# Two tiles alone over all columns, pair operands laid out by sample, and one engine for the pair products' banks

## Chip, cores, metric

The kernel runs on one core of a Trainium2 chip. The metric is the device time of one execution in microseconds. Before the change the median of 3 runs is 491.37 us (489.37 to 493.07). TensorE multiplies, VectorE and ScalarE work elementwise, GpSimd issues the gathers, and SyncE's queue issues the other transfers.

## The reference, cut to what matters

```python
field_idx = jnp.arange(26)
sparse_embed = emb_tables[field_idx[None, :], x_sparse]   # [1024, 26, 64]
z = sparse_embed.reshape(1024, 26 * 64)
gram = jnp.einsum('bik,bjk->bij', sparse_embed, sparse_embed)
inner = gram[:, iu, ju]                                   # 325 pairs i < j
dnn_in = jnp.concatenate([x_dense, z, inner], axis=-1)    # [1024, 13 + 1664 + 325 = 2002]
h = jax.nn.relu(dnn_in @ w1 + b1)                         # w1 [2002, 2002]
out = jax.nn.sigmoid(h @ w2 + b2)                         # w2 [2002, 1]
```

All inputs are fp32. Each sample gathers 26 rows of 64 numbers. The pairwise dot products of those rows, the rows themselves and 13 dense features are the input of a layer of 2002 x 2002 and then of one output.

## The kernel before

**Tiling.** The 1024 samples are eight tiles of 128. The 2002 columns of w1 are two halves of 1002 columns (502 + 500, with two columns shared). The contraction of 2002 rows and the bias is 16 pieces of 128: k = 0 to 12 are z (two fields each), k = 13 to 15 are the *tail* (325 pairs, 13 dense features, a one for the bias). To keep fp32 accuracy each operand is split into a high and a low part of type f32r, and TensorE does three products: x_hi x w_hi, x_hi x w_lo, x_lo x w_hi (lines 361, 362, 345).

**Steps and turns.** A *step* is two tiles and one half: its four accumulators fill four PSUM banks, acc0 to acc3. There are 8 steps. A *turn* is what TensorE does with one piece of weights. Most turns are twelve matmuls (two tiles, two chunks of columns, three products). Step 0 is different: its first 11 pieces are used for tile 0 alone and then loaded again for tile 1 alone (22 turns of six matmuls), since tile 1 is gathered later. That gives 139 turns (TURN, line 63).

**Weights.** SyncE loads a piece into one of four slots of w_raw (line 225), ScalarE rounds it to w_hi (line 396), VectorE subtracts for w_lo (line 474); both have six slots. ScalarE and VectorE do this four turns ahead of its use (LEAD).

**What a tile goes through besides.** Five kinds of parts, written as letters in the code:
- T: GpSimd gathers one field of 128 samples in one indirect transfer (line 267); TensorE transposes them two fields at a time into a side bank (line 297), ScalarE writes x_hi from it (line 401), VectorE x_lo (line 481). In four batches a tile.
- O: operands for the pair products. ScalarE writes the high half of the partitions of pair_u and pair_v (lines 412, 413), VectorE the low half (lines 495, 497).
- G: pair products. One matmul takes four samples at once, 4 samples x 32 fields as weights and 4 x 26 as moving operand (line 312). Four matmuls fill a side bank, eight banks make a tile. The banks are evicted, only the diagonal blocks, by ScalarE (even banks, line 425) and VectorE (odd banks, line 509), four copies each.
- R: VectorE transposes the products in blocks of 32 x 32 and adds the two halves into the tail with 25 short additions (lines 520, 524).
- X: TensorE transposes the tail, ScalarE and VectorE split it.

There are four side banks, used in turn; a part that writes one waits until the fourth use before it has been read.

**Order.** Nothing is scheduled at run time. The table PLAN gives every part a place: the whole number is the turn after whose multiply TensorE does it, a fraction under .5 is early, others late. On ScalarE and VectorE the early parts of turn u come before the splits that `ahead(u)` lists for that turn, the late ones behind them. Every engine runs its queue strictly in order. WARM places short matmuls that produce nothing.

## Time and profile before

| | |
|---|---|
| median of 3 runs | 491.37 us (489.37 to 493.07) |
| profiled execution | 491.99 us, span 490.2 us |
| mean granted clock of TensorE | 0.965 |
| TensorE busy | 464.1 us, 95% |
| VectorE busy | 324.7 us, 66% |
| ScalarE busy | 251.0 us, 51% |
| GpSimd busy | 243.3 us, 50% |
| loaded from HBM | 77.87 MB |

How to read it: the span is the time from the first to the last instruction of the profiled execution. Busy is the time in which an engine executes; TensorE's matmuls overlap, so the distance of their starts says more than their duration. A row names the line of the kernel, the engine, the operation and the tiles it writes and reads. PEclk is the clock granted to TensorE, 1.00 is 2.4 GHz and 0.50 is 1.2 GHz.

### The profile page before, as it was taken

To read this page: it belongs to the slowest core of one execution; us is meant where nothing else is said; L and a number is where in the kernel's file an instruction comes from. 1 tells how busy PE (TensorE), PEld (TensorE's weight loads), DVE (VectorE), ACT (ScalarE), POOL (GpSimd) and SP (SyncE) were. 2 spreads that over 40 slices of the span, in tenths; PEclk is the share of its full clock that TensorE was granted. 3 is DMA by queue.
4 is the path that set the end of the run, shared out by engine and by line. 5 is a ranking of instruction groups with operands and counts; after the bars stand their busy time and mean duration, and the time that the engine had idled before them with its cause. 6 is when DMAs were issued, how large, how long until landed. Compare 5 with 4: busy or idle time off the path is not lost.

```text
span 490.2 us, 6190 instructions
## 1 busy us (share of the span) xinstructions
PE 464.1 (95%) x2113; PEld 396.6 (81%) x2113; DVE 324.7 (66%) x724; ACT 251.0 (51%) x438; POOL 243.3 (50%) x215
## 2 busy tenths in 40 slices
PE   8669888999999999999999999999999999999996
PEld 8557876978888888888878888889788878888884
DVE  3457698678575975787577677876876694446422
ACT  2457558448352854385537553764386443433311
POOL 5777787778788888778788878200000000000000
PEclk9889699689989999998999999999999999999999
DMA  6968657655756775487546855562546347556400
GB/s 158 269 188 242 148 136 217 163 109 130 189 129 170 207 190 129 122 208 203 130 114 173 234 140 149 158 218 84 161 149 180 93 156 246 167 164 212 150 3 0
DMA packets 28751, 78.29 MB, mean 160 GB/s; under 512 B 7696, under 2 KB 7704, under 8 KB 28720
## 3 DMA queue, kind: packets, MB, share of 16 engines
q1 hardware_dynamic: 22064, 71.07, 46.2%
q0 software_dynamic: 6656, 6.83, 11.5%
q8 instruction: 17, 0.28, 0.2%
q14 instruction: 14, 0.11, 0.1%
HBM read 77.87 MB, written 0.00 MB: 159 GB/s over the span
## 4 chain that ended last, share of the span: by engine, by line
PE 71%; POOL 16%; issue 6%; DVE 5%; DMA 1%; ACT 0%; ACTq 0%
PE acc L361 20%; PE acc L362 20%; PE acc L345 20%; POOL z L267 16%; PE side L312 9%; PE side L297 2%; DVE tail L524 1%; DVE square L520 1%; DVE gram L509 1%; DMA z<-in_L_rec_emb_tables_dram,idx 1%; DMA idx<-in_r_x_sparse_dram 1%; DVE weighed L552 1%; PE side L322 1%; ACT L449 0%; DVE w_lo L474 0%
## 5 line engine op out<-in xcount | busy, mean ns | idle before, releaser
L267 POOL DMA_INDIRECT z<-in_L_rec_emb_tables_dram,idx x208 | 242.4, 1165 | 66.5 <-issue 63.1
L361 PE MATMUL acc<-w_hi,x_hi 128*128 128x502 f32 (+3 forms) x512 | 208.0, 406 | 1.4 <-ACT x_hi L401 1.3
L362 PE MATMUL acc<-w_lo,x_hi 128*128 128x502 f32 (+3 forms) x512 | 203.0, 396 | 0.0
L474 DVE TENSOR_TENSOR w_lo<-w_raw,w_hi 128x1002 fp32r<-128x1002 f32 (+1 forms) x139 | 164.1, 1201 | 45.1 <-ACT w_hi L396 44.0
L396 ACT CAST w_hi<-w_raw 128x1002 fp32r<-128x1002 f32 (+1 forms) x139 | 140.3, 1031 | 52.2 <-PE acc L345 47.1
L345 PE MATMUL acc<-w_hi,x_lo 128*128 128x502 f32 (+3 forms) x512 | 145.6, 395 | 0.0
L361 PEld LDWEIGHTS acc<-w_hi,x_hi 128*128 128x128 f32 (+1 forms) x512 | 99.1, 194 | 21.1 <-issue 1.9
L345 PEld LDWEIGHTS acc<-w_hi,x_lo 128*128 128x128 f32 (+1 forms) x512 | 98.7, 193 | 20.4
L362 PEld LDWEIGHTS acc<-w_lo,x_hi 128*128 128x128 f32 (+1 forms) x512 | 98.8, 193 | 18.3
L312 PEld LDWEIGHTS side<-pair_v,pair_u 128*128 128x128 f32 x256 | 67.5, 346 | 2.4 <-issue 1.5
L509 DVE COPY gram<-side 32x104 f32<-32x104 f32 x128 | 33.5, 262 | 52.9 <-PE side L312 51.6
L312 PE MATMUL side<-pair_v,pair_u 128*128 128x104 f32 x256 | 66.6, 438 | 1.1 <-DVE pair_v L497 1.1
L425 ACT COPY gram<-side 32x104 f32<-32x104 f32 x128 | 30.6, 239 | 71.3 <-PE side L312 70.2
L401 ACT CAST x_hi<-side 128x512 fp32r<-128x512 f32 (+2 forms) x32 | 16.2, 507 | 74.4 <-PE side L297 74.3
L481 DVE TENSOR_TENSOR x_lo<-side,x_hi 128x512 fp32r<-128x512 f32 (+2 forms) x32 | 18.8, 590 | 37.6 <-ACT x_hi L401 37.4
L412 ACT ACTIVATE pair_v<-x_hi 64x512 fp32r<-64x512 f32 (+2 forms) x64 | 35.1, 549 | 0.4
L413 ACT CAST pair_u<-x_hi 64x512 fp32r<-64x512 f32 (+2 forms) x64 | 33.5, 524 | 0.0
L552 DVE SCALAR_TENSOR_TENSOR weighed<-acc,w2b 128x502 f32<-128x502 f32 (+1 forms) x32 | 20.7, 677 | 16.7 <-PE acc L345 16.6
L297 PE MATMUL side<-ident,z 128*128 128x128 f32 x104 | 17.5, 287 | 12.5 <-DMA z<-in_L_rec_emb_tables_dram,idx 12.5
L495 DVE CAST pair_u<-x_lo 64x512 fp32r<-64x512 f32 (+2 forms) x64 | 27.9, 437 | 1.4
L297 PEld LDWEIGHTS side<-ident,z 128*128 128x128 f32 x104 | 13.4, 147 | 17.8 <-DMA z<-in_L_rec_emb_tables_dram,idx 14.8
L497 DVE CAST pair_v<-x_hi 64x512 fp32r<-64x512 f32 (+2 forms) x64 | 26.7, 417 | 0.0
(33 smaller groups left out, 111.0 us busy)
## 6 DMA issues: line engine op xcount, KB each, us to landing
w_raw<-in_L_rec_w_dram SPq DMA_DIRECT2D x131, 501.0 KB, 4.3
z<-in_L_rec_emb_tables_dram,idx POOLq DMA_INDIRECT x208, 4.0
w_raw<-in_L_rec_w_dram SPq DMA_DIRECT2D x8, 270.1 KB
w2b<-in_L_rec_w_dram SPq DMA_DIRECT2D x1, 501.0 KB, 7.0
w2b<-in_L_rec_w_dram SPq DMA_DIRECT2D x1, 500.0 KB, 8.9
w_raw<-in_L_rec_w_dram SPq DMA_DIRECT2D x8, 50.9 KB
w_raw<-in_L_rec_b_dram SPq DMA_DIRECT2D x8, 3.9 KB
idx<-in_r_x_sparse_dram SPq DMA_DIRECT2D x1, 104.0 KB, 2.7
```

The costliest lines, as they stand in the source:

```text
L267: pool.indirect_dma_start(out=z[:, t % 2, K * f:K * (f + 1)], out_offset=None, in_=emb_rows, in_offset=bass.IndirectOffsetOnAxis(ap=idx[:, ...
L297: last = nc.tensor.transpose(bank(("T", t, q))[:, P * j:P * (j + 1)], z[:, t % 2, P * (first + j):P * (first + j + 1)], ident[:])
L312: last = nc.tensor.matmul(bank(("G", t, q))[0:SIDES * QUAD, wide * g:wide * (g + 1)], pair_u[:, :, :, b].rearrange("p s f -> p (s f)"), pa ...
L345: last = nc.tensor.matmul(o, x_lo[0:rows, t % XS, k, :], wh, start=False, stop=k == KT - 1)
L361: nc.tensor.matmul(o, hi, wh, start=k == 0, stop=False)
L362: nc.tensor.matmul(o, hi, wl, start=False, stop=False)
L396: nc.scalar.copy(w_hi[0:rows, slot, :], w_raw[0:rows, m % RAW, :]).then_inc(w_hi_done, 1)
L412: nc.scalar.mul(pair_v[0:K, f, :], high, 0.5)
L413: last = nc.scalar.copy(pair_u[0:K, :, f, :].rearrange("p s f b -> p f s b"), high.rearrange("p f (s b) -> p f s b", s=SIDES))
L425: last = nc.scalar.copy(gram[rows, at, :], of.rearrange("p (m j) -> p m j", m=GB)[:, :, FIELDS * s:FIELDS * (s + 1)])
L474: nc.vector.tensor_tensor(w_lo[0:rows, slot, :], w_raw[0:rows, m % RAW, :], w_hi[0:rows, slot, :], ALU.subtract).then_inc(w_lo_done, 1)
L509: last = nc.vector.tensor_copy(gram[rows, at, :], of.rearrange("p (m j) -> p m j", m=GB)[:, :, FIELDS * s:FIELDS * (s + 1)])
```

## The change

Three things are changed.

1. **Steps.** Tiles 0 and 1 are each a step of their own over both halves: one tile, four chunks of columns, again four accumulators and twelve matmuls a turn. A piece of weights is then 2002 columns wide and is loaded and split in one go. The other six tiles go in pairs and by halves as before. There are 128 turns: 32 wide and 96 as before. w_raw has six half slots in place of four, so it holds three wide pieces or six narrow ones, like w_hi and w_lo. Wide pieces are split two turns ahead of their use, narrow ones four. Tile 0 is transposed in eight batches (1, 1, 2, 2, 2, 2, 2, 1 pieces), the others in batches of 4, 4, 4 and 1. The WARM matmuls are gone; 36 matmuls in place of 48 stand before the first turn.
2. **Pair operands.** pair_u and pair_v are laid out by sample: for each of 32 groups of four samples, 128 numbers in a row (4 samples x 32 places, of which 26 are fields and six are zero). A pair product reads both operands packed and writes 128 columns instead of 104. The copies that write the operands (O) read x_hi and x_lo with a stride and write four fields next to each other.
3. **Eviction.** ScalarE evicts all eight banks of a tile. VectorE evicts none.

The table PLAN is written anew. The diff, cut to its core:

```diff
-    BATCHES = [(0, 3), (3, 4), (7, 4), (11, FP - 11)]
+    SOLO = 2
+    STEPS = [([t], list(range(HALVES))) for t in range(SOLO)]
+    STEPS += [([g + b for b in range(GROUP)], [h]) for g in range(SOLO, TILES, GROUP) for h in range(HALVES)]
+    PARTED = [(0, 4), (4, 4), (8, 4), (12, FP - 12)]
+    BATCHES = [PARTED] * TILES
+    BATCHES[0] = [(0, 1), (1, 1), (2, 2), (4, 2), (6, 2), (8, 2), (10, 2), (12, FP - 12)]
...
-    RAW = 4
+    RAW = 6
     SPL = 6
-    ALONE = 11
-    WARM_UP = 48
-    LEAD = 4
+    WARM_UP = 36
...
-    STEPS = HALVES * TILES // GROUP
-    TURN = [(0, k, [t]) for t in range(GROUP) for k in range(ALONE)]
-    TURN += [(0, k, list(range(GROUP))) for k in range(ALONE, KT)]
-    for n in range(1, STEPS):
-        TURN += [(n, k, [n // HALVES * GROUP + b for b in range(GROUP)]) for k in range(KT)]
+    TURN = [(n, k) for n in range(len(STEPS)) for k in range(KT)]
     TURNS = len(TURN)
+    WIDE = [len(STEPS[n][1]) for n, _ in TURN]
+    START = [sum(WIDE[:m]) for m in range(TURNS + 1)]
+    def before(m, ring):
+        last = START[m + 1] - 1 - ring
+        return max([u for u in range(m) if START[u] <= last], default=-1)
...
-        ([-1, 2, 6, 10], [0.5, 3.5, 7.5, 10.1],
-         [10.6, 10.6, 10.6, 10.6, 10.6, 10.6, 10.6, 10.6], [12.5], [13.5]),
-        ([10.8, 13, 16, 19], [11.6, 14.5, 18.5, 21.1],
-         [21.5, 21.5, 21.5, 21.5, 21.6, 21.6, 21.6, 21.6], [22.8], [23.7]),
-        ([22.8, 22.9, 24.9, 26.9], [24.3, 26, 27, 29],
-         [30.1, 30.1, 31.1, 31.1, 32.1, 32.1, 32.1, 32.1], [33.1], [35.5]),
...
+        ([-1, 0, 1, 2, 4, 6, 8, 9], [4.5, 7, 10, 10.5],
+         [10.6, 10.6, 10.6, 10.6, 10.6, 10.6, 11, 11], [11.5], [12.1]),
+        ([13, 15, 18, 19], [15.5, 17.5, 20, 21],
+         [22, 22, 22.5, 22.5, 23, 23, 23.5, 23.5], [24.5], [26]),
+        ([26, 28, 29, 30], [28.5, 30.5, 32, 33],
+         [34, 34, 34.5, 34.5, 35, 35, 35.5, 35.5], [36.5], [38]),
...
-    WARM = [(2.1, 5), (6.1, 5), (10.2, 9), (12.2, 1), (13.1, 5), (17.1, 4), (20.1, 6), (21.1, 5),
-            (23.2, 8)]
...
-        pair_u = sb("pair_u", [P, SIDES, QUAD, APART], f32r)
-        pair_v = sb("pair_v", [P, FIELDS, P], f32r)
+        pair_u = sb("pair_u", [P, APART, SIDES, QUAD], f32r)
+        pair_v = sb("pair_v", [P, APART, SIDES, QUAD], f32r)
...
-        w_raw = sb("w_raw", [P, RAW, HW], fp32)
-        w_hi = sb("w_hi", [P, SPL, HW], f32r)
-        w_lo = sb("w_lo", [P, SPL, HW], f32r)
+        w_raw = sb("w_raw", [P, RAW * HW], fp32)
+        w_hi = sb("w_hi", [P, SPL * HW], f32r)
+        w_lo = sb("w_lo", [P, SPL * HW], f32r)
...
-            return [m for m in range(2, TURNS) if max(m - LEAD, 0) == u]
+            return [m for m in range(1, TURNS) if max(m - 2 * HALVES // WIDE[m], before(m, SPL) + (before(m, SPL) >= 0)) == u]
...
+        def pieces(n):
+            tiles, halves = STEPS[n]
+            pairs = [(t, h, c) for h in halves for c in range(len(CW)) for t in tiles]
+            return [(j, t, h, c) for j, (t, h, c) in enumerate(pairs)]
+        def spot(pairs, k, par, q):
+            first, n = PARTED[q]
+            at = QUAD // 2 * par + first
+            return pairs[k:k + K, :, :, at:at + n].rearrange("p m s f -> p s m f")
+        def operand(x, t, par, q):
+            first, n = PARTED[q]
+            return x[K * par:K * (par + 1), t % XS, first:first + n, :].rearrange("p f (s m) -> p s m f", s=SIDES)
+        def covered(t, q):
+            first, n = PARTED[q]
+            return max(i for i, (k, _) in enumerate(BATCHES[t]) if k < first + n)
+        def wanted(t, q, s):
+            of = bank(("G", t, q))[QUAD * s:QUAD * (s + 1), :].rearrange("p (m c) -> p m c", c=P)
+            of = of[:, :, QUAD * s:QUAD * (s + 1)].rearrange("p m (r k) -> p m r k", r=2)
+            rows, at = placed(q, s)
+            return gram[rows, at, :].rearrange("p m (k r) -> p m r k", r=2), of[:, :, :, 0:FP]
...
-                wide = SIDES * FIELDS
                 for g in range(GB):
-                    b = GB * q + g
                     last = nc.tensor.matmul(
-                        bank(("G", t, q))[0:SIDES * QUAD, wide * g:wide * (g + 1)],
-                        pair_u[:, :, :, b].rearrange("p s f -> p (s f)"),
-                        pair_v[:, :, b:P:APART].rearrange("p f s -> p s f"), start=True, stop=True)
+                        bank(("G", t, q))[:, P * g:P * (g + 1)],
+                        pair_u[:, GB * q + g, :, :].rearrange("p s f -> p (s f)"),
+                        pair_v[:, GB * q + g, :, :].rearrange("p s f -> p (s f)"), start=True, stop=True)
...
+                for j, t, h, c in todo:
+                    o, wh, wl = chunk(j, h, c)
+                    if k == 0 and n >= 1:
...
             def pair_operands(t, q):
-                first, n = BATCHES[q]
                 if q == 0 and t >= 1:
                     act.wait_ge(gram_made, GBANKS * t)
-                act.wait_ge(x_hi_done, count("TX", ("T", t, q)))
+                act.wait_ge(x_hi_done, count("TX", ("T", t, covered(t, q))))
                 for par in range(2):
-                    f = slice(2 * first + par, 2 * (first + n), 2)
-                    high = x_hi[K * par:K * (par + 1), t % XS, first:first + n, :].bitcast(fp32)
-                    nc.scalar.mul(pair_v[0:K, f, :], high, 0.5)
-                    last = nc.scalar.copy(pair_u[0:K, :, f, :].rearrange("p s f b -> p f s b"),
-                                          high.rearrange("p f (s b) -> p f s b", s=SIDES))
+                    high = operand(x_hi, t, par, q).bitcast(fp32)
+                    nc.scalar.mul(spot(pair_v, 0, par, q), high, 0.5)
+                    last = nc.scalar.copy(spot(pair_u, 0, par, q), high)
                 last.then_inc(pairs_act, 1)
             def read_pairs(t, q):
-                if q % 2 == 0:
-                    if q == 0 and t >= 1:
-                        act.wait_ge(turned, t)
-                    act.wait_ge(gram_made, GBANKS * t + q + 1)
-                    for s in range(SIDES):
-                        of = bank(("G", t, q))[QUAD * s:QUAD * (s + 1), 0:SIDES * FIELDS * GB]
-                        rows, at = placed(q, s)
-                        last = nc.scalar.copy(
-                            gram[rows, at, :],
-                            of.rearrange("p (m j) -> p m j", m=GB)[:, :, FIELDS * s:FIELDS * (s + 1)])
-                    last.then_inc(gram_act, 1)
+                if q == 0 and t >= 1:
+                    act.wait_ge(turned, t)
+                act.wait_ge(gram_made, GBANKS * t + q + 1)
+                for s in range(SIDES):
+                    to, of = wanted(t, q, s)
+                    last = nc.scalar.copy(to, of)
+                last.then_inc(gram_act, 1)
...
-            for m in range(2):
-                split_piece(m)
+            split_piece(0)
...
-            nc.vector.memset(pair_u[:, :, FIELDS:QUAD, :].bitcast(fp32), 0.0).then_inc(pad_zero, 1)
+            for pairs in (pair_u, pair_v):
+                pads = pairs[:].bitcast(fp32).rearrange("p m s (r k) -> p (m s) r k", r=2)
+                last = nc.vector.memset(pads[:, :, :, FP:], 0.0)
+            last.then_inc(pad_zero, 1)
...
                 for par in range(2):
-                    f = slice(2 * first + par, 2 * (first + n), 2)
-                    part = slice(K * par, K * (par + 1))
-                    low = x_lo[part, t % XS, first:first + n, :]
-                    nc.vector.tensor_copy(pair_u[K:2 * K, :, f, :].rearrange("p s f b -> p f s b"),
-                                          low.rearrange("p f (s b) -> p f s b", s=SIDES))
-                    last = nc.vector.tensor_copy(pair_v[K:2 * K, f, :],
-                                                 x_hi[part, t % XS, first:first + n, :])
+                    nc.vector.tensor_copy(spot(pair_u, K, par, q), operand(x_lo, t, par, q))
+                    last = nc.vector.tensor_copy(spot(pair_v, K, par, q), operand(x_hi, t, par, q))
...
-                dve.wait_ge(gram_act, gram_counts(GBANKS * (t + 1))[0])
-                dve.wait_ge(gram_dve, gram_counts(GBANKS * (t + 1))[1])
-                nc.vector.transpose(square[:], gram[:].rearrange("p m j -> p j m")).then_inc(turned, 1)
+                dve.wait_ge(gram_act, GBANKS * (t + 1))
+                nc.vector.transpose(square[:].rearrange("p j (k r) -> p j r k", r=2),
+                                    gram[:].rearrange("p (r m) j -> p j r m", r=2)).then_inc(turned, 1)
```

What the table does shows in the order of instructions. **ScalarE, tile 1, around the turns in which its z is transposed** (x_hi is the T part, w_hi a split of weights, pair_u and pair_v the O part, gram the eviction). Before, turns 10 to 14:

```order
L401 CAST x_hi<-side 128x384
L396 CAST w_hi<-w_raw 128x1002
L412 ACTIVATE pair_v<-x_hi 64x3x128
L413 CAST pair_u<-x_hi 64x3x4x32
L412 ACTIVATE pair_v<-x_hi 64x3x128
L413 CAST pair_u<-x_hi 64x3x4x32
L396 CAST w_hi<-w_raw 128x1002
L401 CAST x_hi<-side 128x512
L396 CAST w_hi<-w_raw 128x1002
L432 CAST x_hi<-side 128x384
```

Now, turns 12 to 17:

```order
L417 CAST w_hi<-w_raw 128x2002
L423 CAST x_hi<-side 128x512
L417 CAST w_hi<-w_raw 83x2002
L417 CAST w_hi<-w_raw 128x2002
L423 CAST x_hi<-side 128x512
L417 CAST w_hi<-w_raw 128x2002
L432 ACTIVATE pair_v<-x_hi 64x4x32x4
L433 CAST pair_u<-x_hi 64x4x32x4
L432 ACTIVATE pair_v<-x_hi 64x4x32x4
L433 CAST pair_u<-x_hi 64x4x32x4
L417 CAST w_hi<-w_raw 128x2002 x2
```

The T parts now stand directly ahead of the split of a wide piece that is used two turns later. Before, the split behind them was of a narrow piece, used four turns later.

**ScalarE, the operands and banks of tile 3.** Before, turns 43 to 47:

```order
L412 ACTIVATE pair_v<-x_hi 64x2x128
L413 CAST pair_u<-x_hi 64x2x4x32
L412 ACTIVATE pair_v<-x_hi 64x2x128
L413 CAST pair_u<-x_hi 64x2x4x32
L396 CAST w_hi<-w_raw 128x1002 x2
L425 COPY gram<-side 32x104 x4
L396 CAST w_hi<-w_raw 128x1002
L425 COPY gram<-side 32x104 x4
L396 CAST w_hi<-w_raw 128x1002
L425 COPY gram<-side 32x104 x4
L396 CAST w_hi<-w_raw 128x1002
```

Now, turns 39 to 42:

```order
L417 CAST w_hi<-w_raw 128x1002
L432 ACTIVATE pair_v<-x_hi 64x4x32
L433 CAST pair_u<-x_hi 64x4x32
L432 ACTIVATE pair_v<-x_hi 64x4x32
L433 CAST pair_u<-x_hi 64x4x32
L442 COPY gram<-side 32x4x2x13 x8
L417 CAST w_hi<-w_raw 128x1002
L442 COPY gram<-side 32x4x2x13 x16
L417 CAST w_hi<-w_raw 128x1002
L442 COPY gram<-side 32x4x2x13 x8
L417 CAST w_hi<-w_raw 128x1002
```

Between two splits there were four evictions; now there are eight or sixteen, and the last operand copies stand right ahead of the first of them.

**VectorE, tile 5, turns 57 to 63 of the change** (x_lo is the T part, weighed the second layer of a finished step):

```order
L529 TENSOR_TENSOR x_lo<-side,x_hi 128x384
L497 TENSOR_TENSOR x_lo<-side,x_hi 128x512
L490 TENSOR_TENSOR w_lo<-w_raw,w_hi 128x1002
L507 COPY pair_u<-x_lo 64x4x32x4
L508 COPY pair_v<-x_hi 64x4x32x4
L507 COPY pair_u<-x_lo 64x4x32x4
L508 COPY pair_v<-x_hi 64x4x32x4
L490 TENSOR_TENSOR w_lo<-w_raw,w_hi 128x1002
L497 TENSOR_TENSOR x_lo<-side,x_hi 128x128
L490 TENSOR_TENSOR w_lo<-w_raw,w_hi 128x1002
L546 SCALAR_TENSOR_TENSOR weighed,parts<-acc,w2b 128x502 x2
L546 SCALAR_TENSOR_TENSOR weighed,parts<-acc,w2b 128x500 x2
```

Tile 5's T and O parts share these turns with the tail of tile 4 (just ahead of these rows) and the second layer of step 3.

## Rows read from the trace of the kernel before

**Rows 1.** The page: span; busy us (share of the span) xinstructions.
```profile
span 490.2 us, 6190 instructions
PE 464.1 (95%) x2113; PEld 396.6 (81%) x2113; DVE 324.7 (66%) x724; ACT 251.0 (51%) x438; POOL 243.3 (50%) x215
```

**Rows 2.** Busy time by stretch: stretch, its length, busy us (x), PEclk, DMA share, GB/s.
```profile
core 0: us, PE busy (x) PEld busy (x) DVE busy (x) ACT busy (x) POOL busy (x), PEclk, DMA share, GB/s
0.00:171.60 171.60, 152.96 (x733) 132.57 (x734) 118.12 (x271) 95.60 (x174) 132.39 (x123) 0.91 0.67 175
171.60:486.00 314.40, 310.91 (x1380) 263.92 (x1378) 206.18 (x452) 153.73 (x263) 110.94 (x93) 0.99 0.54 153
```

**Rows 3.** Order of time, TensorE: start us, us, instruction. Turns begin here.
```profile
171.63 0.39 PE L361 MATMUL acc<-w_hi,x_hi 128*128 128x502 f32 x1
...
422.42 0.39 PE L361 MATMUL acc<-w_hi,x_hi 128*128 128x502 f32 x1
...
425.15 0.39 PE L361 MATMUL acc<-w_hi,x_hi 128*128 128x502 f32 x1
```

**Rows 4.** The chain that ended last: first gathers of tiles 0 and 1.
```profile
5.11 1.10 POOL z L267
...
41.48 0.95 POOL z L267
```

**Rows 5.** Busy time by stretch: the densest ten microseconds of transfers.
```profile
10.00:20.00 10.00, 5.73 (x45) 5.24 (x45) 0.56 (x1) 1.36 (x3) 7.56 (x8) 0.95 0.98 316
```

**Rows 6.** Order of time, TensorE: pair products, transpositions, WARM matmuls.
```profile
50.12 8.40 PE L312 MATMUL side<-pair_v,pair_u 128*128 128x104 f32 x32 [1.09 <-DVE pair_v L497]
...
65.86 0.60 PE L297 MATMUL side<-ident,z 128*128 128x128 f32 x4
66.30 1.28 PE L290 MATMUL side<-ident 128*128 128x128 f32 x10
...
127.70 2.07 PE L312 MATMUL side<-pair_v,pair_u 128*128 128x104 f32 x8
129.58 0.45 PE L361 MATMUL acc<-w_hi,x_hi 128*128 128x502 f32 x1
```

**Rows 7.** Busy time by stretch, inside the first burst of pair products.
```profile
53.00:58.00 5.00, 5.00 (x21) 5.00 (x21) 2.57 (x10) 2.40 (x10) 3.78 (x5) 0.51 0.55 126
```

**Rows 8.** Groups by shape: xcount | busy us, mean ns | idle before, us.
```profile
L474 DVE TENSOR_TENSOR w_lo<-w_raw,w_hi 128x1002 fp32r<-128x1002 f32 x131 | 154.9, 1201 | 41.0 <-ACT w_hi L396 39.9
L396 ACT CAST w_hi<-w_raw 128x1002 fp32r<-128x1002 f32 x131 | 132.5, 1031 | 48.7 <-PE acc L345 43.7 <-DMA w_raw<-in_L_rec_w_dram 3.7
L345 PEld LDWEIGHTS acc<-w_hi,x_lo 128*128 128x128 f32 x480 | 92.6, 193 | 19.1
L312 PEld LDWEIGHTS side<-pair_v,pair_u 128*128 128x128 f32 x256 | 67.5, 346 | 2.4 <-issue 1.5
L425 ACT COPY gram<-side 32x104 f32<-32x104 f32 x128 | 30.6, 239 | 71.3 <-PE side L312 70.2
L413 ACT CAST pair_u<-x_hi 64x512 fp32r<-64x512 f32 x32 | 19.3, 604 | 0.0
L520 DVE STREAM_TRANSPOSE square<-gram 128x832 f32<-128x832 f32 x8 | 14.7, 1834 | 0.0
L495 DVE CAST pair_u<-x_lo 64x512 fp32r<-64x512 f32 x32 | 13.6, 425 | 0.7
L481 DVE TENSOR_TENSOR x_lo<-side,x_hi 128x512 fp32r<-128x512 f32 x16 | 11.0, 689 | 13.9 <-ACT x_hi L401 13.8
L552 DVE SCALAR_TENSOR_TENSOR weighed<-acc,w2b 128x500 f32<-128x500 f32 x16 | 10.5, 676 | 0.0
L401 ACT CAST x_hi<-side 128x512 fp32r<-128x512 f32 x16 | 9.4, 587 | 25.1 <-PE side L297 25.0
```

**Rows 9.** Order of time, VectorE: the additions of one tail.
```profile
246.74 2.40 DVE L524 TENSOR_TENSOR tail<-square 128x25 f32<-128x25 f32 x25
```

190 lines of the change are left out of this document (82 added, 108 removed), and 20 rows, old and new, of the table PLAN.

## The prediction

> **What bounds the kernel now.** I read the page first: the span is 490.2 us, and the profiled execution took 491.99 us with what lies around it, 0.6 us over the median of the three runs (491.37), so sums against it carry over as they stand. TensorE is busy for 95% of it, VectorE for 66%, ScalarE for 51% [rows 1]. That average hides two stages, so the second view is the busy time by stretch [rows 2]. In the first 171.6 us, which is all of steps 0 and 1 (tiles 0 and 1 complete, plus the pair products of tile 2), TensorE is busy for 89% at a granted clock of 0.91. From 171.6 us on it is busy for 99% at 0.99: there nothing but TensorE's own work counts. The third view is the order of time. Step 2 begins at 171.63 us, and a plain turn of twelve wide matmuls (one piece of weights, two tiles) takes 425.15 - 422.42 = 2.73 us [rows 3], 0.227 us each. The first stage is paced by GpSimd's gathers: the 26 of a tile take 41.48 - 5.11 = 36.4 us [rows 4], while half the columns of a tile ask only 16 x 1.36 = 22 us of TensorE.
>
> **Part 1, tiles 0 and 1 alone over all columns.** The matmuls stay 1536. The first two steps issue 32 turns of twelve where there were 22 of six and 21 of twelve; both come to 384 matmuls, 87 us. The weights loaded and split rise from 139 half pieces to 32 whole and 96 half, that is 160 halves: 21 more, or 10.5 MB. Price of a whole piece (2002 columns): on VectorE 1002 columns take 1201 ns and 512 take 689 [rows 8], 1.045 ns a column, so 2.25 us; on ScalarE 1031 and 587 ns, 0.906 ns a column, so 1.94 us. The transfer of 1.03 MB at the 316 GB/s of the densest stretch [rows 5] is 3.2 us. All but the last lie under 2.73 us, so on paper a wide turn can run at TensorE's pace once gathers are ahead; at gather pace (two a turn, 2.8 us) it is also close.
>
> What decides is the order on ScalarE. A whole piece is now queued two turns ahead (it was four pieces). Where a transposition is placed early after turn u, ScalarE first waits for it, and only then splits the piece of turn u+2. From the end of multiply u: four transpositions 0.44, 0.2 to ScalarE, x_hi 0.59, split 1.94, then VectorE's 2.25, together 5.4 us [rows 6, 8]; multiply u+1 covers 2.73 and the transpositions 0.44, so TensorE stands about 2.2 us. Today four smaller pieces are ahead, so no such stand appears.
>
> Tile 0: its first transposition goes after two gathers instead of six, so turn 0 starts near 12 us, not 19.3. Turns 0 to 9 hold seven such transpositions, with shorter forms (about 5.0 us a turn), and three others at the transfer's 3.2 to 3.5: 46 us, turn 10 starts at 58. Behind it all 32 pair products wait for the last operand copies, with two splits before them on each engine (about 8 us of standing, from those copies and splits one after the other). Then ScalarE evicts eight banks at 4 x 0.239 = 1.0 us each, 8 us, and VectorE makes the tail, 1.83 + 2.40 us [rows 8, 9]. Two multiplies (5.5 us) hide in that, and the transposed tail and split behind it take 5 us more: turn 13 starts at about 86.
>
> Turns 13 to 31: 19 x 2.73 = 52; nine transposition batches (four of tile 1, four of tile 2, one of tile 3) at 0.44 + 2.2 = 24; pair products of tile 1, 3.7; its tail, 2; operand copies that come before a split (2.5 us on ScalarE), not hidden on some six turns, 5 in all. Sum 87, so step 2 starts at about 174. That is **2.5 us later** than 171.6, and tile 2's pair products are not yet in it.
>
> **Part 2, sample-major operands.** A pair product now costs (129.58 - 127.70) / 8 = 0.235 us [rows 6]. At half the clock 32 of them took 8.40 us, 0.26 each [rows 6, 7], while wide matmuls nearly double there; so the array's columns do not set it. Its two operands do: both step 128 bytes from column to column. The weight load shows 346 ns against 193 for packed operands [rows 8]. Packed 128 x 128 transpositions and warm-ups go at 0.11 us ((66.30 - 65.86) / 4) [rows 6]. I take 0.115; the bounds are 0.06 (a plain share of the 0.227 of 502 columns) and 0.235 (nothing gained). After the start of step 2 there were 5 tiles x 32 x 0.235 = 37.6 us, and will be 6 x 32 x 0.115 = 22.1: **-15.5 us**.
>
> The stride has moved to the copies that write the operands. They read fp32 512 bytes apart, four at a time. For VectorE no row has such a read; the nearest is the transpose with a stride of 104 bytes, 1834 ns for 832 elements [rows 8], two cycles each, where packed subtractions take one. A copy of 64x512 takes 425 ns now. Bounds are 0.42 (stride free) and 1.2 (two cycles on one port); I take 0.68, twice the slope, since this copy runs at two elements a cycle now. Twelve of them and four small ones a tile: 9.3 us, against 6.8. For ScalarE no row reads with a stride; bounds 0.61 (as now) and 1.03 us; I take 0.61, the value of its present rows.
>
> The Trainium skill ("Advanced Engine Details and Errata", SBUF Cachelines) says that accesses which each fall on another 16-byte line pay a penalty, and names no engine as exempt. The weight load and the transpose above agree. Taken for ScalarE as well, it would give 521 us, the fourth case below; taken for no copy, 491, the second.
>
> **Part 3, ScalarE evicts all.** VectorE loses 128 copies (33.5 us), ScalarE gains 128 (30.6). The averages stay low, near 300 and 335 us of 500. It counts in turns 31 to 44, where tiles 2 and 3 now both have their copies, products and tails. TensorE: 14 x 2.73 + 64 x 0.115 + 2 = 47.7 us. ScalarE: 14 splits 14.4, 16 evictions 15.7, operand copies 12.1, the rest 3.1: 45.3. VectorE: splits 16.8, copies 13.2, x_lo 3.5, two transposes and tails 8.6, second layer 4 x 0.75 [rows 8] = 3: 45.1. Three engines at 95% with waits for each other don't overlap fully: I put 4 at the change of step, 7 ahead of tile 3's products (its last operand copies stand half a turn before them), 4 at the two tails, **+15**. In turns 56 to 63 VectorE has 8 splits, tile 5's x_lo and copies, tile 4's tail and a second layer, 29 us against 23 of TensorE: +6, and +4 for the same pile in tiles 6 and 7, **+10**.
>
> Hidden at no cost: 12 fewer warm-ups and the padding memsets (before the first gather lands), 10.5 MB more to load (after step 1 the queue is idle half the time).
>
> **Sum.** 491.99 + 2.5 - 15.5 + 15 + 10 = **504 us**.
>
> **The cases.**
> 1. As summed, 504 us, 498 to 513. Chance 0.40.
> 2. The operand copies cost what they cost now. Turn 40's wait and the pile at 56 to 63 shrink by 13 us: 491. For it: two elements a cycle may hide the stride. Against: the transpose row. 0.20.
> 3. Faster: the splits keep up. If they run beside the multiplies, the chain of 5.4 us vanishes and the busiest engine sets turns 13 to 31. That is VectorE: 21 splits 43, x_lo 6, operand copies 15, a tail 4, a second layer 3, together 71 us instead of 87, and in tile 0 some 6 us come back in the same way: 482. For it: averages are far from full. Against: only one multiply lies beside the chain. It decides where a wide turn with a transposition takes under about 4.3 us. 0.14.
> 4. ScalarE pays for the stride as well: 13.9 us a tile instead of 8.4. In turns 31 to 44 it has 53 us against TensorE's 48, and pair products wait everywhere for pairs_act: +17, 521 us. 0.18.
> 5. Pair products don't get faster, because a short matmul has a floor that these rows don't show: six tiles x 32 x 0.12 = 23 less what the waits absorb: 525. The change would then not do what its first half is for. 0.08.
>
> Within 1% is 487 to 496.5 us, about what a measurement of this kernel can tell. Faster by over 1%: case 3, 0.14. Within: case 2, 0.20. Slower: cases 1, 4 and 5, 0.66. The range 484 to 528 leaves out most of case 3 and the upper ends of 4 and 5, together under 0.2. It takes in both bounds of VectorE's copy but for the 1.2 us one (over 540), which I hold for improbable.
>
> **What would show it.** Step 2's first matmul near 174 us (case 3: near 152). Pair products at 0.11 to 0.12 each. The 64x512 operand copies at 0.68 on VectorE and 0.61 on ScalarE. Between turns 13 and 31 TensorE idle ended by VectorE's w_lo, some 2 us after each batch of transpositions; a wait of 5 us or more ahead of tile 3's pair products; granted clock at half after the long stands of tile 0. The forecast is wrong in its mechanism if TensorE is busy for 95% or more of turns 13 to 31, or if the copies show no change.

## The result and the profile after

| | before | after |
|---|---|---|
| median | 492.22 us (489.37 to 495.07, 4 runs) | 534.5 us (533.27 to 541.95, 4 runs) |
| ratio | | **1.085** (1.077 to 1.093) |
| span of the profiled execution | 490.2 us | 531.4 us |
| TensorE, VectorE, ScalarE busy | 464, 325, 251 us | 443.5, 334.5, 349.1 us |

The kernel is 42 us slower. The forecast was slower by 13, with a range of 484 to 528. One run of the changed kernel, 541.95 us at a lower clock, is left out of the ratio; all ratios below are of such fast runs alone. The page of the changed kernel, as [rows 1]:

```profile
span 531.4 us, 5897 instructions
PE 443.5 (83%) x1993; PEld 363.4 (68%) x1993; DVE 334.5 (63%) x590; ACT 349.1 (66%) x559; POOL 267.3 (50%) x215
...
PE 50%; ACT 24%; DVE 12%; issue 8%; DMA 4%; POOL 3%; SPq 0%; ACTq 0%; DVEq 0%
```

TensorE has 20 us less to do and takes 41 us longer: it stands. The last line is the chain that ended last; ScalarE and VectorE hold 36% of it. Groups by shape, as [rows 8] (count, busy us, mean ns, idle before):

```profile
L490 DVE TENSOR_TENSOR w_lo<-w_raw,w_hi 128x2002 fp32r<-128x2002 f32 x30 | 67.1, 2246 | 45.5 <-ACT w_hi L417 45.4
L417 ACT CAST w_hi<-w_raw 128x2002 fp32r<-128x2002 f32 x30 | 55.6, 1868 | 5.4 <-DMA w_raw<-in_L_rec_w_dram 5.2
L432 ACT ACTIVATE pair_v<-x_hi 64x512 fp32r<-64x512 f32 x48 | 54.1, 1128 | 0.3
L433 ACT CAST pair_u<-x_hi 64x512 fp32r<-64x512 f32 x48 | 53.2, 1109 | 0.0
L334 PEld LDWEIGHTS side<-pair_v,pair_u 128*128 128x128 f32 x256 | 36.6, 215 | 23.5 <-issue 20.9 <-ACT gram L442 0.9
L508 DVE CAST pair_v<-x_hi 64x512 fp32r<-64x512 f32 x48 | 34.8, 726 | 0.0
L507 DVE CAST pair_u<-x_lo 64x512 fp32r<-64x512 f32 x48 | 34.1, 710 | 1.1
```

The wide splits (2.25 and 1.87 us) and VectorE's operand copy (0.72, forecast 0.68) came as priced. ScalarE's copy did not: **1.12 us where 0.61 was taken**, 96 times. The pair products got cheap, as [rows 6]; eight of them, then a multiply:

```profile
283.18 1.08 PE L334 MATMUL side<-pair_v,pair_u 128*128 128x128 f32 x8 [0.31 <-issue]
284.10 0.44 PE L384 MATMUL acc<-w_hi,x_hi 128*128 128x502 f32 x1
```

(284.10 - 283.18) / 8 = 0.115 us each. ScalarE's busy time was forecast near 300 us and is 349.1; 96 copies at 0.51 us more are those 49. Where TensorE waits (us in all, times, longest; "issue" is a wait for which the profile shows no releaser), first before, then after:

```profile
PE side L297 <- DMA z<-in_L_rec_emb_tables_dram,idx: 12.5, 6, 4.8
PE side L322 <- DVE tail L524: 4.8, 4, 1.8
```

```profile
PE acc L384 <- DVE w_lo L490: 23.9, 11, 5.7
PE acc L384 <- DVE weighed L546: 14.3, 4, 7.4
PE side L344 <- DVE tail L521: 12.8, 4, 7.1
PE side L334 <- issue: 11.0, 3, 7.9
PE side L334 <- DVE pair_v L508: 7.9, 1, 7.9
```

Before, TensorE waited for gathers. Now it waits for the two engines that prepare its operands. The 7.9 us put down to "issue" are ahead of tile 3's products at 232.23 us; VectorE's last operand copy of that tile ends at 232.13, so this too is a wait for the copies. Busy time by stretch, as [rows 2], cut at steps 2 and 3:

```profile
0.00:189.60 189.60, 136.26 (x568) 109.63 (x569) 119.63 (x166) 119.66 (x157) 152.68 (x116) 0.87 0.70 211
189.60:262.20 72.60, 59.01 (x278) 48.25 (x276) 47.34 (x111) 57.18 (x114) 54.60 (x51) 0.90 0.60 149
262.20:531.00 268.80, 248.19 (x1149) 205.47 (x1149) 167.54 (x315) 172.23 (x289) 60.03 (x50) 0.96 0.49 141
```

Step 2 starts 18 us late (its first multiply stands at 189.78 us, before at 171.63). Turns 32 to 47 take 72.5 us (the 16 turns of step 2 took 55.2). From turn 48 to the start of the last turn it takes 261.6 us (255.8).

**An account of TensorE.** A *stand* is a time in which TensorE issues nothing. From the starts of its matmuls I sorted each distance by the matmul at which it begins and by the clock; over 0.7 us counts as a stand.

| us | before | after | difference |
|---|---|---|---|
| stands | 25.6 | 92.9 | +67 |
| multiplies, without stands | 361 | 378 | +17 |
| pair products | 62 | 33 | -29 |
| transpositions, WARM | 36 | 22 | -14 |

Multiplies follow each other at 0.228 us at the full clock (2.4 GHz), 0.418 at half (1.2 GHz). Before, 43 distances lay at half, after 131: 88 x 0.19 = 17 us, which is the second line. The four differences add up to the 41 us by which the span grew. Half the clock was granted for 91 us in place of 36 (some 2 us of each lie behind the last instruction). In the changed kernel each such spell begins during a stand or within 1.3 us behind one, but not every stand has one: the two of 2.8 us ahead of the tails at 218 and 252 us have none. The long stand ahead of tile 0's products, and the stretch of time behind it (PEclk is the third number from the end):

```profile
60.69 1.09 PE L369 MATMUL acc<-w_hi,x_lo 128*128 128x502 f32 x4
69.68 0.66 PE L334 MATMUL side<-pair_v,pair_u 128*128 128x128 f32 x2 [7.90 <-DVE pair_v L508]
```

```profile
70.00:80.00 10.00, 10.00 (x46) 9.26 (x46) 0.00 (x0) 6.57 (x27) 7.56 (x9) 0.63 0.36 85
```

In the kernel before, 27 of the 34 us at half clock within the span lay elsewhere: in four spells that began within bursts of the strided pair products or within 1 us behind one. The second burst of 32 ran from 87.3 to 95.5 us, with no stand near it:

```profile
90.00:100.00 10.00, 10.00 (x34) 9.14 (x34) 7.01 (x21) 3.92 (x13) 7.87 (x8) 0.53 0.48 103
```

**What the stands of turns 13 to 31 are made of.** There are ten, of 1.3 to 5.9 us, 25.8 us in all. First one behind operand copies, ahead of turn 18. Order of time: TensorE, ScalarE, VectorE.

```profile
113.57 1.07 PE L369 MATMUL acc<-w_hi,x_lo 128*128 128x502 f32 x4
117.72 0.46 PE L384 MATMUL acc<-w_hi,x_hi 128*128 128x502 f32 x1 [3.08 <-DVE w_lo L490]
```

```profile
109.14 1.14 ACT L432 ACTIVATE pair_v<-x_hi 64x512 fp32r<-64x512 f32 x1
110.19 1.08 ACT L433 CAST pair_u<-x_hi 64x512 fp32r<-64x512 f32 x1
111.28 1.12 ACT L432 ACTIVATE pair_v<-x_hi 64x512 fp32r<-64x512 f32 x1
112.30 1.10 ACT L433 CAST pair_u<-x_hi 64x512 fp32r<-64x512 f32 x1
113.42 3.62 ACT L417 CAST w_hi<-w_raw 128x2002 fp32r<-128x2002 f32 x2
```

```profile
112.89 0.72 DVE L507 CAST pair_u<-x_lo 64x512 fp32r<-64x512 f32 x1
113.53 0.75 DVE L508 CAST pair_v<-x_hi 64x512 fp32r<-64x512 f32 x1
115.33 4.40 DVE L490 TENSOR_TENSOR w_lo<-w_raw,w_hi 128x2002 fp32r<-128x2002 f32 x2 [1.05 <-ACT w_hi L417]
```

ScalarE copies for 4.3 us before it comes to the split. VectorE is through with its own copies and waits 1.05 us. TensorE starts when the first whole w_lo is there, at 115.33 + 2.25 = 117.6.

Four others, ahead of turns 15, 17, 20 and 30 (1.9 to 2.5 us), are the prediction's chain behind a T part. Ahead of turn 30: transposition at 169.67, x_hi at 170.30, split at 170.79, w_lo at 172.69, multiply at 175.08, 5.4 us as forecast. The longest, ahead of turn 31, is a third kind. TensorE waits for w_lo, VectorE for ScalarE, and ScalarE for the load of the piece:

```profile
183.86 0.76 PE L384 MATMUL acc<-w_hi,x_hi 83*128 83x502 f32 x1 [5.67 <-DVE w_lo L490]
179.58 1.86 ACT L417 CAST w_hi<-w_raw 83x2002 fp32r<-83x2002 f32 x1 [2.29 <-DMA w_raw<-in_L_rec_b_dram]
```

Its three transfers were issued from 165.99 us on. The prediction had the loads as hidden. The traces of the changed kernel and of all runs with part 1 (e5 and e8 apart, see there) show this wait at turn 31, of 1.9 to 6.0 us; the kernel before has none behind 90 us. What makes the load late is open.

In the later steps the pile stands on VectorE. At turn 64 TensorE waits for the second layer, which stands behind tile 5's copies and splits:

```profile
320.65 0.76 PE L384 MATMUL acc<-w_hi,x_hi 128*128 128x502 f32 x1 [7.39 <-DVE weighed L546]
```

```profile
316.55 0.70 DVE L508 CAST pair_v<-x_hi 64x512 fp32r<-64x512 f32 x1
317.28 1.20 DVE L490 TENSOR_TENSOR w_lo<-w_raw,w_hi 128x1002 fp32r<-128x1002 f32 x1
318.40 0.28 DVE L497 TENSOR_TENSOR x_lo<-side,x_hi 128x128 fp32r<-128x128 f32 x1
318.60 1.19 DVE L490 TENSOR_TENSOR w_lo<-w_raw,w_hi 128x1002 fp32r<-128x1002 f32 x1
319.71 0.67 DVE L546 SCALAR_TENSOR_TENSOR weighed<-acc,w2b 128x502 f32<-128x502 f32 x1
```

### The profile page after: what moved, and what is told of

Its sections match the earlier page's. It is cut to its first block, busy times and chain, and to the rows that moved or that the text cites. A ratio compares the mean times of both kernels' runs of the same rounds, so it can differ in the third digit from the quotient of the medians.

```text
span 531.4 us, 5897 instructions
## 1 busy us (share of the span) xinstructions
PE 443.5 (83%) x1993; PEld 363.4 (68%) x1993; DVE 334.5 (63%) x590; ACT 349.1 (66%) x559; POOL 267.3 (50%) x215
## 4 chain that ended last, share of the span: by engine, by line
PE 50%; ACT 24%; DVE 12%; issue 8%; DMA 4%; POOL 3%; SPq 0%; ACTq 0%; DVEq 0%
PE acc L384 15%; PE acc L385 14%; PE acc L369 14%; ACT w_hi L417 9%; ACT pair_v L432 5%; DVE w_lo L490 5%; ACT pair_u L433 5%; PE side L334 4%; ACT gram L442 4%; POOL z L297 3%; DMA w_raw<-in_L_rec_b_dram 2%; DVE tail L521 2%; DVE square L516 2%; PE side L321 1%; DVE pair_u L507 1%
## 5 line engine op out<-in xcount | busy, mean ns | idle before, releaser
L490 DVE TENSOR_TENSOR w_lo<-w_raw,w_hi 128x1002 fp32r<-128x1002 f32 (+3 forms) x128 | 185.7, 1462 | 150.3 <-ACT w_hi L417 149.8
L384 PE MATMUL acc<-w_hi,x_hi 128*128 128x500 f32 (+3 forms) x512 | 218.2, 426 | 46.3 <-DVE w_lo L490 23.9
L385 PE MATMUL acc<-w_lo,x_hi 128*128 128x500 f32 (+3 forms) x512 | 211.1, 412 | 0.0
L417 ACT CAST w_hi<-w_raw 128x1002 fp32r<-128x1002 f32 (+3 forms) x128 | 157.0, 1241 | 40.6 <-PE acc L369 28.4
L369 PE MATMUL acc<-w_hi,x_lo 128*128 128x500 f32 (+3 forms) x512 | 146.8, 402 | 0.0
L432 ACT ACTIVATE pair_v<-x_hi 64x512 fp32r<-64x512 f32 (+1 forms) x64 | 61.0, 953 | 0.4
L433 ACT CAST pair_u<-x_hi 64x512 fp32r<-64x512 f32 (+1 forms) x64 | 60.1, 939 | 0.0
L334 PE MATMUL side<-pair_v,pair_u 128*128 128x128 f32 x256 | 36.7, 296 | 19.6 <-issue 11.0
L507 DVE CAST pair_u<-x_lo 64x512 fp32r<-64x512 f32 (+1 forms) x64 | 39.7, 620 | 1.4
L508 DVE CAST pair_v<-x_hi 64x512 fp32r<-64x512 f32 (+1 forms) x64 | 40.3, 630 | 0.0
L321 PE MATMUL side<-ident,z 128*128 128x128 f32 x104 | 18.5, 288 | 3.1 <-DMA z<-in_L_rec_emb_tables_dram,idx 3.1
```

The lines of the kernel that those rows point to most:

```text
L334: last = nc.tensor.matmul(bank(("G", t, q))[:, P * g:P * (g + 1)], pair_u[:, GB * q + g, :, :].rearrange("p s f -> p (s f)"), pair_v[:, GB ...
L369: last = nc.tensor.matmul(o, x_lo[0:rows, t % XS, k, :], wh, start=False, stop=k == KT - 1)
L384: nc.tensor.matmul(o, hi, wh, start=k == 0, stop=False)
L385: nc.tensor.matmul(o, hi, wl, start=False, stop=False)
L417: nc.scalar.copy(w_hi[0:rows, slice(*columns(m, SPL))], w_raw[0:rows, slice(*columns(m, RAW))]).then_inc(w_hi_done, 1)
L432: nc.scalar.mul(spot(pair_v, 0, par, q), high, 0.5)
```

## The experiments

Ratios are to the kernel before on the same chip. The last four columns are of the profiled execution: start of step 2, the 16 turns from there (32 to 47 in the new numbering), from there to the start of the last turn ("48-127"), time at half clock (some 2 us of it behind the last instruction). The profiled executions of e16 and e18 took 5 us more than their medians. One trace a kernel is no measure of its scatter: turn 13 starts at 91.3 us in the changed kernel and at 94.3 and 95.9 in e3 and e2, e2's plan being the same up to there.

| run | median us | ratio (95%) | step 2 | 32-47 | 48-127 | half |
|---|---|---|---|---|---|---|
| before | 492.22 | 1 | 171.6 | 55.2 | 255.8 | 36 |
| after | 534.5 | 1.085 (1.077 to 1.093) | 189.8 | 72.5 | 261.6 | 91 |
| e1 ScalarE packed | 522.5 | 1.062 (1.058 to 1.065) | 187.5 | 73.8 | 251.1 | 88 |
| e2 late T | 535.23 | 1.088 (1.084 to 1.092) | 187.4 | 74.5 | 261.8 | 106 |
| e3 swapped | 533.5 | 1.082 (1.078 to 1.086) | 192.3 | 73.8 | 258.7 | 106 |
| e4 parts 1, 2 | 530.55 | 1.072 (1.066 to 1.078) | 189.4 | 71.4 | 260.9 | 101 |
| e9 part 1 | 527.81 | 1.075 (1.070 to 1.080) | 182.9 | 73.3 | 259.6 | 64 |
| e10 part 2 | 491.4 | 0.996 (0.991 to 1.000) | 175.3 | 54.2 | 250.6 | 55 |
| e12 part 3 | 499.45 | 1.013 (1.006 to 1.020) | 177.1 | 56.9 | 258.7 | 51 |
| e11 long fillers | 548.88 | 1.115 (1.111 to 1.120) | 198.4 | 78.6 | 262.6 | 42 |
| e13 fillers | 527.89 | 1.071 (1.066 to 1.077) | 187.3 | 72.4 | 255.9 | 48 |
| e14 both packed | 508.84 | 1.030 (1.024 to 1.036) | 184.2 | 70.7 | 244.8 | 71 |
| e15 halves | 526.11 | 1.068 (1.062 to 1.074) | 181.2 | 72.6 | 261.7 | 88 |
| e16 part 2, late G | 492.57 | 0.997 (0.994 to 1.000) | 179.6 | 53.9 | 254.6 | 65 |
| e17 three together | 486.63 | 0.987 (0.984 to 0.990) | 163.9 | 70.6 | 245.0 | 30 |
| e18 part 2 packed | 472.5 | 0.957 (0.952 to 0.962) | 172.5 | 51.9 | 244.2 | 41 |

### e1 and e14: the stride of the operand copies

```diff
+        def packed(x, t, par, q):
+            first, n = PARTED[q]
+            flat = x[K * par:K * (par + 1), t % XS, first:first + n, :].rearrange("p f b -> p (f b)")
+            return flat.rearrange("p (s m f) -> p s m f", s=SIDES, f=n)
...
-                    high = operand(x_hi, t, par, q).bitcast(fp32)
+                    high = packed(x_hi, t, par, q).bitcast(fp32)
```

e1 does it for ScalarE's copies alone, e14 for both engines'.

> The changed kernel, but ScalarE's operand copies read x_hi packed (same number of elements, same places written; the operands therefore hold the wrong samples, which is the part of the computation that is changed). Stride theory: the 64x512 copies fall from 1.11 to about 0.6 us, ScalarE's busy time by some 45 us, and about 20 of the 42 us by which the change is slower come back: about 513 us. Rival (the order of wide splits and transpositions stands, whatever the copies cost): the copies get cheaper but the time stays within 6 us of 534.

> The changed kernel with the operand copies of both engines reading packed (they take the wrong samples; the writes and all else stay), asked again on another occasion. e1 (ScalarE's alone) gave back 12 us. Theory A, the stride is dear on both engines: VectorE's copies fall from 0.72 to 0.45 us (48 x 2 x 0.27 = 26 us of its time), 6 to 10 us more than e1, 513 to 517 us. Theory B, only ScalarE is late: 520 to 524 us, as e1. In both the loss of part 1 stays: over 510 us.

In e14 the copies of 64x512 are back at the price that they had before the change:

```profile
L437 ACT ACTIVATE pair_v<-x_hi 64x512 fp32r<-64x512 f32 x48 | 30.2, 629 | 0.3
L438 ACT CAST pair_u<-x_hi 64x512 fp32r<-64x512 f32 x48 | 29.0, 604 | 0.0
L512 DVE CAST pair_u<-x_lo 64x512 fp32r<-64x512 f32 x48 | 20.3, 424 | 1.1
L513 DVE CAST pair_v<-x_hi 64x512 fp32r<-64x512 f32 x48 | 20.0, 417 | 0.0
```

e1 gave back 12 us, less than its theory's 20. e14 gave back 26, more than either of its theories. 17 of them lie in turns 48 to 127, where the stands fall from 17.5 to 5.9 us, and 5.6 before step 2. ScalarE's stride is not the only one that counts; VectorE's is worth as much again. In turns 13 to 31 the stand ahead of turn 18 falls from 3.5 to 1.5 us, but the stands there stay at 26 us in all: with the copies out of its way ScalarE waits 5.7 us in place of 2.3 for the load of turn 31's piece. The 64x128 copies stay at 0.43 us on ScalarE; a copy of one field alone still writes with a stride.

### e3: the stride on the other side

```diff
+        def spot_w(pairs, k, par, q):
+            first, n = PARTED[q]
+            at = QUAD // 2 * par + first
+            return pairs[k:k + K, :, :, at:at + n].rearrange("p m s f -> p f s m")
...
-                    last = nc.scalar.copy(spot(pair_u, 0, par, q), high)
+                    last = nc.scalar.copy(spot_w(pair_u, 0, par, q), high)
```

The read has its fields outermost in the same way: it is packed, and the write takes steps of 512 bytes. Same values at the same places.

> The changed kernel, but all operand copies run through the same elements in the other order: fields outermost, samples innermost. They read packed and write with a stride of 512 bytes; the operands hold the same numbers as in the change. If only a read with a stride costs: the 64x512 copies take 0.6 us on ScalarE and about 0.42 on VectorE, and the total is near 500. If a stride costs on either side: 1.1 and 0.7 us, as in the change, 534. No row so far tells these apart.

```profile
L441 ACT ACTIVATE pair_v<-x_hi 64x512 fp32r<-64x512 f32 x48 | 54.0, 1125 | 0.3
...
L517 DVE CAST pair_v<-x_hi 64x512 fp32r<-64x512 f32 x48 | 37.9, 789 | 0.0
```

Nothing is won, as its second theory had it: the price is the stride's, read or written.

### e2: the hand-over chain

```diff
-        ([13, 15, 18, 19], [15.5, 17.5, 20, 21],
+        ([13.5, 15.5, 18.5, 19.5], [15.5, 17.5, 20.5, 21],
```

and so for the T parts of tiles 2 and 3 that lie in turns 26 to 31: behind the splits of their turn, no longer ahead of them.

> The changed kernel, but in turns 13 to 31 the transposition batches are placed late instead of early, so that ScalarE and VectorE split the wide piece of two turns later before they wait for the transposition. Hand-over theory (the term of 2.2 us for each of nine batches in the prediction): some 20 us come back, step 2 starts near 170 us and the total is near 515. Stride theory: the engines' load sets those turns, so only 3 to 6 us come back: 528 to 531.

The time stayed, and neither theory came true. That doesn't clear the chain that my prediction made the stands of (T, x_hi, split, w_lo). In e2's trace its four stands are gone or shorter (ahead of turns 15, 20 and 30 none over 0.7 us, ahead of 17 one of 1.0), and turns 13 to 31 take 91.4 us in place of 98.5. The stand ahead of turn 31 grew from 5.9 to 9.4 us, 6.0 of them ScalarE's wait for the load. Turns 0 to 12 took 4.6 us more with the same plan, which is scatter, and the later turns 2.2 more. So the chain is there at four of nine places, at its forecast price, and the 7 us that its removal gave in this trace were gone by the end.

### e4, e9, e10, e12: the parts apart

e9 is part 1 (the changed kernel with the old operand layout and eviction by both engines), e10 and e12 are parts 2 and 3 on the kernel before, e4 is parts 1 and 2. The eviction of e4 as an example:

```diff
+            def read_pairs(t, q):
...
+                for s in range(SIDES):
+                    to, of = wanted(t, q, s)
+                    last = nc.vector.tensor_copy(to, of)
```

> The changed kernel with the third part undone: VectorE evicts the odd banks again, four copies each, at the same places. Stride theory: ScalarE loses 32 us of work but VectorE, at 0.7 us a copy, gains 33, so 3 to 6 us come back: 528 to 531. Rival (the eviction by one engine makes the waits ahead of and between the pair products): 15 us or more come back, under 520.

> Part 1 of the change alone (tiles 0 and 1 alone over all columns, the new plan; operands by field and eviction by both engines as before), asked again because all kernels of the run before, the kernel before the change too, stood for some 40 us with no engine issuing. Theory A, the whole loss sits in the stands that the new steps and plan bring, and the slow operand copies add to it only later: slower than before by 6 to 8%, 522 to 531 us, since the pair products still cost 0.235 us each while the stands of TensorE are those of the changed kernel (8 us ahead of tile 0's products, 7 ahead of its tail, 6 and 8 in turns 30 and 40). Theory B, the copies of part 2 carry most of the loss: part 1 alone within 2%, 492 to 502 us, step 2 starting before 180 us.

> Part 2 alone on the kernel before (operands by sample, steps, plan and eviction by both engines as before). Theory A: the cheaper pair products (0.235 to 0.112 us, 256 of them, 31 us, of which the waits take back a part) outweigh the dearer copies, which have cover in the old plan: 478 to 488 us, granted clock at half for under 60 us. Theory B, the copies decide: ScalarE gains 48 x 0.5 = 24 us twice over, its splits come late, 500 us or more.

> Part 3 alone on the kernel before (ScalarE evicts all eight banks of a tile's pair products, all else as before), asked again on another occasion. Theory A, ScalarE has room in the old plan (251 us busy of 490, plus 31): within 1% of before, 487 to 497 us. Theory B, the eight evictions in a row, 1.0 us a bank where the banks came free from two engines in turn, pace the pair products, and ScalarE's splits behind them come late: 3% slower as on the disturbed occasion, 505 us.

Part 1 alone costs 7.5%, as its theory A had it; part 3 alone 1.3%, more than its theory A and less than B; part 2 alone nothing that can be told from no change, where its theories had a gain or a loss. e4 came back by 4 us, within its first theory. With part 1 there, parts 2 and 3 add at most another point: the intervals of e9, e4 and the changed kernel overlap. In the changed kernel as in e10, then, part 2's cheap products (29 us less, table above) are paid back by its copies (26 us, e14). Part 1 itself is four things at once, the wide steps, the larger w_raw, the new table and the end of the WARM matmuls, and no run takes the table from the steps. e10 shows how part 2 comes to nothing. Its pair products are cheap, its copies dear, and TensorE waits for these:

```profile
L325 PEld LDWEIGHTS side<-pair_v,pair_u 128*128 128x128 f32 x256 | 35.2, 209 | 16.1 <-ACT pair_u L425 9.6 <-issue 4.9 <-DVE gram L514 0.2
...
L424 ACT ACTIVATE pair_v<-x_hi 64x512 fp32r<-64x512 f32 x32 | 36.5, 1139 | 0.2
```

```profile
PE side L312 <- DMA z<-in_L_rec_emb_tables_dram,idx: 14.4, 4, 5.7
PE side L325 <- ACT pair_u L425: 6.9, 4, 2.3
PE side L325 <- DVE pair_v L504: 4.9, 3, 3.4
```

### e5 to e8: the same questions on a disturbed chip

e5, e6 and e7 are the kernels of e9, e10 and e12, e8 that of e14.

> Part 1 alone: tiles 0 and 1 alone over all columns, with the table, the rings and the batches of the change, but with the operands laid out as before and both engines evicting. If the wide steps are what costs (packing ScalarE's reads gave back only 11 of 42 us), this is slower than before by 20 us or more, 512 to 520, and step 2 starts after 178 us. If the stride of the operand copies is most of it on both engines, this lies within 10 us of the time before: 490 to 500.

> Part 2 alone: the kernel before with the sample-major operands, its own table and both engines evicting. Gain: 256 pair products at 0.112 instead of 0.235 us, 31 us of TensorE. Cost: the operand copies, 1.1 for 0.6 us on ScalarE and 0.7 for 0.42 on VectorE. If the copies' stride decides: slower than before, 498 to 508. If TensorE's saving decides: 465 to 480.

> Part 3 alone: the kernel before, ScalarE evicts all eight banks. VectorE loses 33.5 us of work, ScalarE gains 31; four copies then pass one engine in 1.0 us a bank while a burst of pair products needs 0.94. Expected of every theory: within 1% of before, 490 to 497, tile 0's burst of eight banks some us longer. If single-engine eviction is the brake, above 500.

> The changed kernel with packed reads in the operand copies of both engines (the operands hold the wrong samples: that is the part of the computation changed). VectorE's 64x512 copies fall from 0.72 to 0.42. What part 2 costs in all is then gone and only its gain on TensorE is left. If VectorE's copies matter as much as ScalarE's: 505 to 512. If the wide steps alone hold the rest: 517 to 522, as with ScalarE's copies packed alone.

On this chip the kernel before took 569.59 us. In e6's trace no TensorE, VectorE or ScalarE instruction starts between 18.5 and 61.4 us, while gathers go on; the first multiply behind it:

```profile
62.11 0.76 PE L374 MATMUL acc<-w_hi,x_hi 128*128 128x502 f32 x1 [43.29 <-issue]
```

The ratios were 1.034 (1.028 to 1.041), 0.987 (0.977 to 0.997), 1.029 (1.019 to 1.039) and 1.019 (1.013 to 1.024). Such stretches of over 6 us lie at other places in each of the four traces (84 to 125 us in e5, 70 to 87 besides in e6, 94 to 111 and 239 to 254 in e7, 95 to 119 in e8) and cover other waits. I draw nothing from these four; what made them is open.

### e11 and e13: what the clock costs

```diff
+    WARM = [(10.6, 30), (12.1, 27), (30.4, 22), (40.0, 30), (63.0, 27), (79.0, 17), (95.0, 10)]
```

Matmuls that produce nothing are put into seven long stands (the line is e13's; e11 has twice as many). The kernel before had such matmuls too (WARM); the change had taken them out.

> The changed kernel with matmuls that produce nothing placed in its seven long stands (60 ahead of tile 0's products, 55 ahead of its tail, 45 in turn 30, 60 ahead of tile 3's products, 55, 35 and 20 in turns 63, 79 and 95; 0.11 us each, a little less than the stand). It tells what the granted clock costs by itself. Theory A, the half clock behind each stand is a cost of its own: 131 of 1536 distances of multiplies at 0.418 us in place of 0.228 are 25 us, two thirds of them behind these seven stands, so half clock falls from 91 to about 30 us and the time by 13 to 17 us, to 517 to 521. Theory B, the turns behind a stand wait for ScalarE's and VectorE's splits anyway, so that a faster clock only turns into other stands: half clock falls, the time stays within 4 us of 534.

> The changed kernel with half as many fillers as in e11 (30, 27, 22, 30, 27, 17 and 10 matmuls in the seven long stands), since one filler turned out to be two records of 0.112 us, 0.224 us: now 163 x 0.224 = 37 us, which fit in the 46 us of these stands. Theory A, the half clock is a cost of its own: half clock falls from 91 to 45 us or less, multiplies at 0.418 us from 131 to some 70, which gives back 60 x 0.19 = 11 us: 520 to 526 us. Theory B, a faster clock only lengthens the next wait for a split: within 4 us of 534.

The fillers ahead of tile 0's products, in e11 and in e13 (order of time, TensorE):

```profile
63.53 13.56 PE L320 MATMUL side<-ident 128*128 128x128 f32 x120
```

```profile
61.51 6.86 PE L320 MATMUL side<-ident 128*128 128x128 f32 x60
```

An fp32 matmul is two records of 0.112 us; e11's 60 fillers took 13.6 us where 8 were free, and the kernel became slower by 14 us at nearly full clock. e13's fit: half clock falls from 91 to 48 us, the time by 6.6 us, 1.4 points (the two intervals touch at 1.077). That lies between its theories: A holds at some 0.6 of its 11 us. The forecast had named the half clock, and priced it at nothing.

### e15: whole pieces in two handovers

```diff
-                nc.scalar.copy(w_hi[0:rows, slice(*columns(m, SPL))],
-                               w_raw[0:rows, slice(*columns(m, RAW))]).then_inc(w_hi_done, 1)
+                for i in range(WIDE[m]):
+                    nc.scalar.copy(w_hi[0:rows, parts_of(m, SPL, i)],
+                                   w_raw[0:rows, parts_of(m, RAW, i)]).then_inc(w_hi_done, 1)
```

and so on VectorE; TensorE waits for the half that its next matmul reads.

> The changed kernel with each whole piece split in two handovers (ScalarE rounds the first 1002 columns and signals, VectorE subtracts them while ScalarE rounds the other 1000; TensorE starts a turn on the first half). Loads, ring and plan stay. Theory A, the wait of the whole piece (1.94 + 2.25 us one after the other) makes the stands of turns 13 to 31: waits for w_lo fall from 24 us to under 12, step 2 starts at 176 to 180 in place of 190, the time at 520 to 525. Theory B, those stands are ScalarE's and VectorE's own load (splits, x_hi, copies) and not the handover: with 32 more instructions each at 0.15 us it stays within 5 us of 534.

8.4 us come back, all of them before step 2 (181.2 in place of 189.8): 1.7 points, short of theory A's 10 to 14 and more than B's 5. The waits for w_lo fall only from 23.9 to 20.7 us. The stands ahead of turns 15, 17 and 30 are gone, that ahead of turn 31 grew to 8.4 us, 4.8 of them the wait for the load.

### e16: part 2 with later products

```diff
-         [58.5, 58.5, 59.5, 59.5, 60.5, 60.5, 61.5, 61.5], [62.5], [63.5]),
+         [59.5, 59.5, 60.5, 60.5, 61, 61, 61.5, 61.5], [62.5], [63.5]),
```

and so for tiles 3, 5, 6 and 7.

> The kernel before with part 2 alone (e10, 491.4 us), and in its plan the pair products of tiles 3 to 7 begin one turn later and take two turns less, so that they no longer stand for the operand copies that became longer. e10 showed such stands of 2.2 to 2.7 us ahead of the products of tiles 4, 5, 6 and 1.4 ahead of tile 7. Theory A, the stands were only that: they vanish, 8 us, and a spell of half clock with them: 481 to 486 us, faster than before by 1.2 to 2.2%. Theory B, the stand moves to the tail behind (a turn later too) or to the step's change: within 3 us of 491.

Theory B holds. The waits for ScalarE's pair_u are gone; in their place stand longer ones for the tail (8.8 us), the second layer (6.4) and the gathers (21.0). Room ahead of the products was taken from behind them.

### e17 and e18: do the causes close the account?

e17 is e14 and e15 together, with e13's fillers in five places (30, 27, 22, 20, 15). e18 is e10 with both engines' copies packed.

> The changed kernel with the three suspected costs taken away at once: operand copies of both engines read packed (wrong samples; all else stays), whole pieces handed over in halves, and fillers in the five longest stands (30, 27, 22, 20, 15 matmuls). Theory A, the three are separate costs: 27 + 8 + 7 us less than 534.5, 490 to 497 us, within 1% of before, so they close the account. Theory B, they are the same waits counted more than once (a stand that is gone needs no filler): 500 to 508 us.

> The kernel before with part 2 alone, the operand copies reading packed (wrong samples; all else stays): what the cheaper pair products are worth on the old plan if their operands came without a stride. Theory A, the copies take back what the products give: 256 x (0.235 - 0.112) = 31 us come off TensorE, the waits ahead of the products (5 + 7 us in e10) vanish, 470 to 478 us. Theory B, the gathers and the change of step pace the first stage and only the 5 tiles of the second stage count, 160 x 0.123 = 20 us, in part lost in stands: 478 to 486 us.

e17 ends 48 us below the changed kernel, where the three apart gave 26 + 8 + 7 = 41, and 3 us under its theory A. So they are separate costs. The surplus lies before step 2, which starts 26 us earlier (163.9), where the three apart gave 17. TensorE's waits for w_lo are down from 23.9 to 8.8 us. That one late split makes the next one late would explain it; no run shows it.

The account does not close by this. Turns 32 to 47 take 70.6 us in e17 and 70.7 to 78.6 in all other kernels with part 1, against 51.9 to 56.9 in those without it. Tile 2's pair products and tail are in there now. The old kernel had no stand in these turns. The changed one has 15.1 us of stands and 14 us at half clock there, e17 7.3 and 12. e17 falls under the old time because turns 0 to 31 and 48 to 127 became shorter than they were. That these turns are long comes with part 1; by what in it is open.

e18 gains 4.3%, as its theory A had it: with packed reads part 2 is worth 21 us on the old plan, with strided ones 1 to 2. It lies 14 us below e17, so parts 1 and 3 still cost that much with all three causes gone. Its 64x512 copies took 0.77 and 0.74 us on ScalarE, not 0.63 and 0.60 as in e14: their runs of four fields are written from field 3 or 7 on, not from a multiple of four. Both kernels compute pair products of the wrong samples, so they show a price and are no versions to use. A version of e17 with true operands was not run.

## Why the prediction was wrong

**Direction and most places right, two terms wrong.** The sum was 504; 534.5 was measured. By stage, forecast and measured: step 2's start 174 and 189.8; turns 32 to 47 55.2 + 15 = 70 and 72.5; turns 48 to 127 255.8 - 15.5 + 10 = 250 and 261.6. The steps that failed are the price of ScalarE's strided copy, on which the -15.5 of part 2 rested, and the half clock, which has no term.

- **Part 1, turns 0 to 31 (+2.5; measured +18 in the whole change, +11 with part 1 alone, e9).** Tile 0's part was near: turn 13 at 91.3 where 86 stood. Turns 13 to 31 took 98.5 us in place of 87. The stands were not undersized: nine hand-overs with their transpositions, a tail and copies were put at 31 us; measured are stands of 25.8 and transpositions of 3.6. But the stands have several causes (the chain at four places, copies, evictions at turn 25, one load), where the forecast had mostly the chain. What the sum lacks is the clock: 52 us were put down for 228 multiplies, and those that follow without a stand took 64.6, since 65 of them lay at or near the distance of half clock, 12.7 us more than at the full one. That is the whole miss of these turns. The loads were put down as hidden, and turn 31 waits for one.
- **Part 2 (-15.5; measured 1 to 2 us alone, e10, and no gain from e9 to e4).** The product's price was right (0.115 us). It was set against the copies by one value taken from the wrong end: ScalarE's stride at nothing, "the value of its present rows". Its bounds were 0.61 and 1.03; measured 1.12, above both. The row nearest to it was VectorE's transpose at two cycles an element, and case 4 (521 us) said what follows. The strided copies of both engines cost 26 us (e14), 17 of them in turns 48 to 127, and this with their share of the clock. The Trainium skill ("Advanced Engine Details and Errata", SBUF Cachelines) has accesses that each fall on another 16-byte line pay, and names no engine as exempt. e3 and e14 agree, on both engines and on the read and the write side: 1.13 and 0.79 us with a stride, 0.63 and 0.42 packed.
- **Part 3 and the crowding (+15 and +10).** Turns 32 to 47: 17 us more than before against 15. Turn 64's wait was forecast at 6 and is 7.4 us. Tile 3's products wait 7.9 us (7 forecast). These held in size. That they belong to ScalarE's evictions did not: e4 without part 3 has 71.4 us there, e12 with part 3 alone 56.9. Part 1 alone (e9) has 73.3, so it brings them.
- **The clock.** It was named as a sign and is in no term. It costs 17 us by the distances of multiplies; 7 of them came back by keeping TensorE busy in seven stands (e13).
- **The cases.** Case 4 had the stride right, at 0.18 and with too small a price, since it added 17 us where e14 gave back 26, and reckoned them from turns 31 to 44; its 521 is nearer than the 504 of case 1, and part of that is luck, as it too has no term for the clock. The signs held but for ScalarE's copy and step 2's start: stands of some 2 us behind transpositions (four of nine), 7.9 us ahead of tile 3's products, half clock behind tile 0's long stands.

## What to carry to other kernels

A stride in an operand isn't removed by moving it from one engine to another: price it at its new place at the rate of the nearest strided row, for every engine that takes part, and take the dear end where that engine prepares what the bounding engine waits for. Before a plan that gives an engine its work in larger pieces, add up what stands in its queue between two pieces, not the piece alone, and look at the last load of each step as well. And a long stand can cost twice: once by itself, once at half clock behind it, so a sum of stands needs a term for the clock (here 17 us for 67 us of added stands).

## What the runs showed of the hardware

- A copy of 64x512 fp32 within SBUF took 0.60 to 0.63 us on ScalarE packed and 1.11 to 1.14 with steps of 512 bytes, whether read (after, e10) or written (e3); on VectorE 0.42 and 0.71 to 0.79. Read packed and written in runs of four from field 3 or 7 on (e18), it took 0.74 to 0.77 and 0.44 to 0.47.
- A weight load with a stride of 128 bytes took 346 ns and a pair product 0.235 us; packed 215 ns and 0.115.
- At half the granted clock a multiply of 502 columns follows after 0.418 us in place of 0.228. Pair products of 104 columns with strided operands hardly slow down, 0.26 us for 0.235 [rows 6, 7]; those of 128 columns with packed operands do, 0.21 for 0.11 (after).
- The granted clock fell to 0.53 during and behind 32 strided pair products in a row, with TensorE never idle (before, 90 to 100 us).
- An fp32 matmul of 128 columns is two records and 0.224 us (e11).
- Indirect gathers took 1.28 us each on GpSimd in the changed kernel, 1.17 before, and in its variants 1.17 (e17) to 1.33 (e13); what slows them is open.
